# A macaron stack on one core: how the ternary FFN's weights are split and its chunks ordered, and attention's norm in two parts

## The reference

```
x = x + 0.5 * ffn(ln(x))     # w3(gelu(h2(gelu(h1(silu(w1 x s1) * (w2 x s2))))))
x = x + mamba(ln(x))         # selective scan, 256 channels, 16 states
x = x + 0.5 * ffn(ln(x))     # same weights
x = x + 0.5 * moe(ln(x))     # 16 experts, top 4, and a shared one
x = x + attn(ln(x))          # 16 heads of 64, outliers of the diagonal masked, two softmaxes
x = x + 0.5 * moe(ln(x))     # same weights as the moe above
```

## Time and profile before

| | us |
|---|---|
| median of 3 runs | 2042.3 |
| the profiled execution | 2039.14 |
| its span, first to last instruction | 2037.7 |
| of it PE busy | 1844.3 (91%) |
| DVE, POOL, ACT busy | 1374.8, 1183.9, 1124.5 |

### The profile page before, as it was taken

How to read it: one execution, slowest core, us unless ns; L and a number is a source line. 1 busy time by engine, 2 the same in 40 slices (tenths; PEclk the granted TensorE clock), 3 DMA queues, 4 the chain that set the end, 5 groups by cost and what they waited for, 6 DMA issues and landing times. The chain is left out here.

```text
span 2037.7 us, 21921 instructions
## 1 busy us (share of the span) xinstructions
PE 1844.3 (91%) x7360; PEld 1301.5 (64%) x7360; DVE 1374.8 (67%) x2202; ACT 1124.5 (55%) x1587; POOL 1183.9 (58%) x669
## 2 busy tenths in 40 slices
PE   5998999788997956999999999999999999998588
PEld 3773444335775634777777777777777777765266
DVE  5426899985517753677777777777777777774476
ACT  4326777744326445666566666665666566643444
POOL 2451777863444542466666666665757666668345
PEclk8999999999998978999999999999999999999799
DMA  2000000000001024132223231313131313100100
GB/s 93 0 1 0 0 0 0 1 0 1 0 4 43 1 50 103 34 76 48 67 44 71 43 72 39 76 42 74 38 76 39 76 38 75 38 12 11 52 6 16
DMA packets 46048, 74.51 MB, mean 37 GB/s; under 512 B 26864, under 2 KB 28528, under 8 KB 45680
## 3 DMA queue, kind: packets, MB, share of 16 engines
q1 hardware_dynamic: 43744, 72.35, 15.4%
q10 hardware_dynamic: 2160, 0.77, 0.1%
q0 software_dynamic: 32, 0.00, 0.0%
HBM read 20.93 MB, written 1.18 MB: 11 GB/s over the span
## 5 line engine op out<-in xcount | busy, mean ns | idle before, releaser
L2119 POOL TENSOR_TENSOR at_e_lo<-at_e,at_e_hi 128x1024 fp32r<-128x1024 f32 x256 | 614.7, 2402 | 377.3 <-DVE at_e_hi L2086 375.4
L1944 ACT ACTIVATE at_e<-at_ps 128x1024 f32<-128x1024 f32 x256 | 263.0, 1028 | 281.4 <-PE at_ps L1851 281.4
L1936 ACT ACTIVATE at_ps<-at_ps,at_neg_diag 128x1024 f32<-128x1024 f32 x256 | 278.6, 1088 | 89.2 <-DVE at_neg_diag L2004 89.2
L2011 DVE TENSOR_REDUCE at_row_max<-at_ps 128x1 f32<-128x1024 f32 x256 | 311.2, 1216 | 5.7 <-PE at_ps L1832 5.7
L2086 DVE CAST at_e_hi<-at_e 128x1024 fp32r<-128x1024 f32 x256 | 258.0, 1008 | 35.4 <-ACT at_e L1944 35.1
L2004 DVE CUSTOM_DVE_ANT_0 at_junk_diag<-at_ps,ident 128x128 bf16<-128x128 f32 x256 | 74.1, 290 | 258.8 <-PE at_ps L1805 258.7
L390 POOL TENSOR_TENSOR ffn_lo<-ffn_hid,ffn_hi 128x512 fp32r<-128x512 f32 x96 | 124.6, 1300 | 173.0 <-DVE ffn_hi L317 173.0
L1020 POOL TENSOR_TENSOR mb_work<-mb_work,mb_c 128x1024 f32<-128x1024 f32 x64 | 151.9, 2374 | 98.2 <-DVE mb_work L989 95.9
L1803 PE MATMUL at_ps<-at_k,at_q 128*128 128x512 f32 x512 | 162.0, 398 | 20.7 <-DMA at_k<-at_qk_lo 13.8
L1864 PE MATMUL at_pv_ps<-at_e_hi,at_v_hi 128*128 128x512 f32 x512 | 174.6, 422 | 0.3 <-ACT at_pv_sb L1960 0.3
L1832 PE MATMUL at_ps<-at_k,at_q 128*128 128x512 f32 x512 | 162.6, 399 | 11.3 <-DVE at_row_max L2011 8.0
(11 more groups left out here) (343 smaller groups left out, 3788.4 us busy)
## 6 DMA issues: line engine op xcount, KB each, us to landing
at_q<-at_qk_hi SPq DMA_DIRECT2D x64, 256.0 KB, 3.4
at_k<-at_qk_hi SPq DMA_DIRECT2D x32, 512.0 KB, 5.9
at_q<-at_qk_lo SPq DMA_DIRECT2D x32, 256.0 KB, 6.5
at_k<-at_qk_lo SPq DMA_DIRECT2D x32, 256.0 KB, 6.3
at_recips<-at_recip_row SPq DMA_DIRECT2D x32, 256.0 KB, 3.4
ffn_h_raw<-in_h SPq DMA_DIRECT2D x2, 1024.0 KB, 8.1
at_head_w_raw<-in_w_qkv SPq DMA_DIRECT2D x32, 64.0 KB, 4.2
x<-in_x SPq DMA_DIRECT2D x4, 256.0 KB, 4.8
```

Source lines behind the costliest of these rows:

```text
L1936: act.eng.activation(ps[:], ps[:], ACT.Exp, scale=SCALE, bias=m.small["neg_diag"][s][:, blk:blk + 1], accum_out=m.small["sums"][s][:, blk: ...
L1944: act.eng.activation(m.e[e % 2][:], slot("turned_scores", h, blk)[:], ACT.Exp, scale=SCALE).then_inc(sem["at_exp"])
L2011: dve.eng.tensor_reduce(m.small["row_max"][h % SLOTS][:, blk:blk + 1], slot("best", h, blk)[:], AX.X, ALU.max).then_inc(sem["at_best_out"])
L2119: pool.eng.tensor_tensor(m.e_lo[e % 3][:], m.e[e % 2][:], m.e_hi[e % 3][:].bitcast(F32), ALU.subtract).then_inc(sem["at_lo"])
```

## The change

The arithmetic stays the same; order, engines, queues and waits differ.

FFN, start: w1 and w2 are loaded from ACT's queue, right after the identity, and both are split by POOL (rounding and rest, two operations each). h1 is rounded by ACT after its norm work, and its rest made by POOL in four pieces. h2 and w3 are rounded by ACT after the first and third item of h1, and their rests made by DVE after the third and sixth. Mamba's loads move to SP's queue, behind the FFN's. PE waits for each matrix where it is first read. FFN, order (both FFNs): `j` is outside and `m` inside in every layer, in all the numberings too. DVE finishes and splits chunk 0 before it finishes chunk 1.

Attention: the first part centres all four chunks, and finishes, rounds and splits chunks 0 and 1; the main part then starts. The rest (inverse of chunk 3, finishing and splitting 2 and 3, the value weights) follows head 0's rounding on ACT and DVE, and on POOL it follows head 1's constant rows. PE waits in `project` and `values` for the chunks that they read. PSUM for the norm lies in the main part's banks, so two variances wait until an earlier one is read. SBUF tiles of the main part are allocated in another order.

```diff
 def ffn_u(t, first, m, j):
-    return t * FFN_U + first * KH + m * 2 + j
+    return t * FFN_U + first * KH + j * KH + m
...
 def ffn_pe(c, m_, t):
-    if t == 0:
-        pe.wait_ge(sem["ffn_w_lo"], len(c.ffn_parts))
     for first in range(0, NCH, 2):
-        for m in range(KH):
-            for j in range(2):
+        for j in range(2):
+            for m in range(KH):
                 pe.wait_ge(sem["ffn_xn_lo"], t * NCH + ch + 1)
+                pe.wait_ge(sem["ffn_in_parts"], 2)
...
+                pe.wait_ge(sem["ffn_in_parts"], 4)
...
+            if layer == 0:
+                pe.wait_ge(sem["ffn_in_parts"], 4 + KH)
+            else:
+                pe.wait_ge(sem["ffn_w_lo"], 2)
...
 def ffn_act(c, m_, t):
     if t == 0:
+        act.wait_ge(sem["ffn_h1_load"], 16)
+        act.eng.activation(c.ffn_parts["h1"][0][:], m_.raw["h1"][:], ACT.Copy).then_inc(sem["ffn_w_hi"])
         act.wait_ge(sem["ffn_load"], c.ffn_load_count)
-        for k, (hi, _) in c.ffn_parts.items():
-            act.eng.activation(hi[:], m_.raw[k][:], ACT.Copy).then_inc(sem["ffn_w_hi"])
...
+                    if t == 0 and first == 0 and layer == 0 and slot in FFN_LATE_HI:   # {0: "h2", 2: "w3"}
...
 def ffn_dve(c, m_, t):
     for j in range(2):
         norm_finish(dve, c, n0 + j, m_.norm_ps[j], m_.xn[j], m_.inv[j], m_.sq[j])
-    for j in range(2):
         split_xn(j, j)
...
+                    if t == 0 and first == 0 and layer == 0 and slot in FFN_LATE_LO:   # {2: "h2", 5: "w3"}
...
 def ffn_pool(c, m_, t):
     if t == 0:
-        pool.wait_ge(sem["ffn_w_lo"], len(c.ffn_parts))
+        pool.wait_ge(sem["ffn_in_load"], 2 * 16)
+        for i, k in enumerate(("w1", "w2")):
+            hi, lo = c.ffn_parts[k]
+            pool.eng.tensor_copy(hi[:], m_.raw[k][:]).then_inc(sem["ffn_in_parts"])
+            pool.wait_ge(sem["ffn_in_parts"], 2 * i + 1)
+            pool.eng.tensor_tensor(lo[:], m_.raw[k][:], hi[:].bitcast(F32), ALU.subtract).then_inc(sem["ffn_in_parts"])
+        hi, lo = c.ffn_parts["h1"]
+        pool.wait_ge(sem["ffn_w_hi"], 1)
+        for k in range(KH):
+            pool.eng.tensor_tensor(lo[:, k, :], m_.raw["h1"][:, k, :], hi[:, k, :].bitcast(F32),
+                                   ALU.subtract).then_inc(sem["ffn_in_parts"])
...
 def attention_norm_act(c, m):
+    load_logs(act)
+    for ch in range(2):
+        norm_square(act, c, 12 + ch, m.xn[:, COLS[ch]], m.inv[ch])
+    norm_square(act, c, 14, m.xn[:, COLS[2]], m.inv[2])
+    norm_inverse(act, c, 12, m.var_ps[0], m.inv[0], m.sq[0])
+    norm_inverse(act, c, 13, m.var_ps[1], m.inv[1], m.sq[1])
+    norm_square(act, c, 15, m.xn[:, COLS[3]], m.inv[3])
+    for ch in range(2):
+        attention_round_xn(c, m, ch)
+    norm_inverse(act, c, 14, m.var_ps[2], m.inv[2], m.sq[2])
+
+def attention_later_norm_act(c, m):
+    norm_inverse(act, c, 15, m.var_ps[3], m.inv[3], m.sq[3])
+    for ch in range(2, NCH):
+        attention_round_xn(c, m, ch)
     act.wait_ge(sem["attn_load"], 2 * 16)
     act.eng.activation(m.wv_hi[:], m.wv_raw[:], ACT.Copy).then_inc(sem["at_wv_hi"])
...
     act.wait_ge(sem["at_xn_lo"], NCH)
     act.wait_ge(sem["at_wv_lo"], 1)
...
+def attention_norm_dve(c, m):
+    for ch in range(NCH):
+        norm_centre(dve, c, 12 + ch, m.mean_ps[ch], c.x[:, COLS[ch]], m.xn[:, COLS[ch]])
+    for ch in range(2):
+        norm_finish(dve, c, 12 + ch, m.var_ps[ch], m.xn[:, COLS[ch]], m.inv[ch], m.sq[ch])
+    for ch in range(2):
+        attention_rest_of_xn(c, m, ch)
...
 def project(h):
+        pe.wait_ge(sem["at_xn_lo"], 2 * (h // HEADS) + 2)
...
         if at := due(t, AT_QK + 1):
             round_qk(at[0])
+            if at[0] == 0:
+                attention_later_norm_act(c, m)
```

More of the change, by code:

```diff
@@ L328, in ffn_dve @@
         dve.wait_ge(sem["ffn_load"], c.ffn_load_count)
[L329 to L334, removed]
+        dve.eng.tensor_scalar(c.half_s3[:], c.half_s3[:], 0.5, None, ALU.mult).then_inc(sem["ffn_w_lo"])
+        dve.wait_ge(sem["ffn_w_lo"], 1)
     for first in range(0, NCH, 2):
-        for m in range(KH):
-            for j in range(2):
+        for j in range(2):
+            for m in range(KH):
                 u, v = ffn_u(t, first, m, j), ffn_v(t, first, 0, m, j)
@@ L418, in ffn @@
         m.raw = {}
[L419 to L424 removed]
+        if t == 0:
+            for k, (hi, _) in c.ffn_parts.items():
+                m.raw[k] = sb(f"ffn_{k}_raw", hi.shape, F32)
+            for k in ("w1", "w2"):
+                nc.scalar.dma_start(m.raw[k][:], c.dram[k]).then_inc(c.sem["ffn_in_load"], 16)
+            nc.sync.dma_start(m.raw["h1"][:], c.dram["h1"]).then_inc(c.sem["ffn_h1_load"], 16)
+            for k in ("h2", "w3"):
+                nc.sync.dma_start(m.raw[k][:], c.dram[k]).then_inc(c.sem["ffn_load"], 16)
+                c.ffn_load_count += 16
+            for tile, name in c.mamba_loads:
+                nc.sync.dma_start(tile[:], c.dram[name]).then_inc(c.sem["mamba_load"], 16)
         m.parts = [[(sb(f"ffn_hi{layer}{j}", [P, KH, CH], F32R), sb(f"ffn_lo{layer}{j}", [P, KH, CH], F32R))
@@ L1607, in attention_norm_pe @@
 def attention_norm_pe(c, m):
[L1608 to L1623 removed]
+    pe, sem = c.pe, c.sem
@@ new lines, in attention_norm_pe, with attention_round_xn @@
+    for ch in range(3):
+        norm_mean(pe, c, m.mean_ps[ch], c.x[:, COLS[ch]])
+    for ch in range(2):
+        norm_variance(pe, c, 12 + ch, m.var_ps[ch], m.inv[ch])
+    norm_mean(pe, c, m.mean_ps[3], c.x[:, COLS[3]])
+    for ch in range(2, NCH):
+        pe.wait_ge(sem["norm_done"], 3 * (12 + ch - 2) + 1)
+        norm_variance(pe, c, 12 + ch, m.var_ps[ch], m.inv[ch])
+    pe.wait_ge(sem["norm_centred"], 12 + NCH)
+    pe.wait_ge(sem["at_xn_lo"], 2)
+def attention_round_xn(c, m, ch):
+    act, sem = c.act, c.sem
+    act.wait_ge(sem["norm_done"], 3 * (12 + ch) + 3)
+    act.eng.activation(m.xn_hi[:, COLS[ch]], m.xn[:, COLS[ch]], ACT.Copy).then_inc(sem["at_xn_hi"])
@@ L2112, in attention_pool @@
             fill_spare_rows(c, m, at[0])
+        if (at := due(t, AT_SPLIT)) and at[0] == 1:
+            attention_later_norm_pool(c, m)
         if at := due(t, AT_TURNED, BLK):
@@ L2152, in attention @@
         m.v_hi = sb("at_v_hi", [P, BLK, GROUP, 2, HD], F32R)
+        m.pv_ps = mem.enter_context(nc.psum_tensor("at_pv_ps", [P, 2 * CH], F32))
+        m.ps = [mem.enter_context(nc.psum_tensor(f"at_ps{i}", [P, 2 * CH], F32)) for i in range(3)]
+        m.mean_ps = [m.ps[ch // 2 * 2][:, HALF[ch % 2]] if ch >= 2 else m.pv_ps[:, HALF[ch]] for ch in range(NCH)]
+        m.var_ps = [m.pv_ps[:, HALF[ch % 2]] for ch in range(NCH)]
         with ExitStack() as early:
@@ L2158, in attention @@
             m.sq = [scratch[:, 1, COLS[ch]] for ch in range(NCH)]
-            m.banks = [early.enter_context(nc.psum_tensor(f"at_nps{i}", [P, CH], F32))[:] for i in range(8)]
             attention_norm_sp(c, m)
@@ L2236, in build, with later @@
         with ExitStack() as early:
+            def later(name, shape):
+                tile = sb(name, shape, where=early)
+                c.mamba_loads.append((tile, name))
+                return tile
             shapes = {"w1": [P, HID], "w2": [P, HID], "h1": [P, KH, HID], "h2": [P, KH, HID], "w3": [P, KH, P]}
```

151 lines of the change are left out of this document (73 added, 78 removed).

## The result

The changed kernel takes 2015.44 us, the median of 4 runs (2013.88 to 2017.08); the kernel before, timed beside it, 2043.79 (2041.71 to 2045.34). The ratio is 0.9862, 95% interval 0.9845 to 0.9879. The forecast was 2017, the range 2010 to 2027. By the medians 28.4 us are saved, where 25.5 were forecast. Run again on another chip with the experiments, the changed kernel took 2014.83 against 2042.19, 0.9869 (0.9853 to 0.9886).

The account below looks back on a forecast made before the run. PE's waits at the stage starts and for FFN splits were taken as the bound, attention's middle being PE-busy. Gains of 24.8 us plus about 0.7 for restarts, 25.5 off the 2042.3 median, gave 2017 us, range 2010 to 2027.

Parts of the forecast that it names:

- First FFN's start: First FFN: first gate product at 16.0 in place of 26.68, gate stage ending at 30.7 in place of 39.44, gaining 8.7 us.
- Rival A: First FFN's start: POOL and DVE disturb each other little, so it gains 2 more, 2015 us; chance 0.12.
- Rival B: First FFN's start gains less, since x arrives later or h1 comes late and holds ACT, 2022 us; chance 0.11.
- The table load's term: First FFN's norm: fewer DMA issues on ACT let the table load come earlier, giving 1.3 us.
- Squares: First FFN: squares of the next chunks, delayed by ACT's rounding of h2 and w3, cost 0.2 us.
- Three waits: First FFN: PE's three waits for POOL's `lo` of a hidden block go, 2.5 us.
- Second FFN: Second FFN: starting after chunk 0's split gives 2.1 us, and three waits for `lo` that go give 2.3.
- h2 and w3 later: First FFN: rounding and rests of h2 and w3, about 16 us per engine, hide beside 22.6 us of matmuls, cost zero.
- Attention: Attention's start: projection 0 starts at 744.6 against 752.87, after norming two chunks, gaining 8.2 us.
- Projection at full clock: Attention's start: PE stands still for only 2 us, so the projection's six matmuls run at full clock, saving 1.2 us.
- Room of 2.1 for the second half: Attention: the rest of the norm ends at 757.1, the first score can be read at 759.2, 2.1 us to spare.
- Rival C: Attention: the norm's second half overruns its gap by 5 us, with a cold clock, 2023 us; chance 0.10.

Follow-up runs that it names:

- pool_late: Changed kernel with one wait more: POOL makes the rests of h1 only when chunk 1's norm is split; 2012.21 us, ratio 0.9853 to the kernel before.
- q_act: Changed kernel with the fourteen mamba loads back on ACT's queue, behind w1 and w2, instead of SP's; 2018.05 us, ratio 0.9888 to the kernel before.
- u_order: Changed kernel with the FFN's blocks going in pairs of chunks again, in both FFNs; 2026.29 us, ratio 0.9928 to the kernel before.
- d_attn: Kernel before with only attention's part of the change: norm in two parts, tiles in their new places; 2031.81 us against 2041.08, ratio 0.9953.
- place: Kernel before with only the order in which attention's tiles take their places in SBUF changed; 2042.31 us against 2041.08, ratio 1.0003.
- warm1: Changed kernel with five unread matmuls in attention's norm, two ahead of variances, three ahead of the projection; 2013.82 us, ratio 0.9860 to the kernel before.
- slack: Changed kernel with nine unread DVE passes ahead of the second half of attention's norm; 2018.10 us, ratio 0.9884 to the kernel before.
- a_again: The changed kernel, unchanged, timed and profiled once more; 2014.83 us against 2042.19 for the kernel before, ratio 0.9869.
- combo: Changed kernel with POOL's h1 rests held until chunk 1 is split, and unread matmuls in attention's gaps; 2009.87 us, ratio 0.9849 to the kernel before.
- combo_f: Same as combo, with four more unread matmuls ahead of the first FFN's first gate matmul; 2009.10 us, ratio 0.9841 to the kernel before.

## Why the prediction was right

The mechanisms were right but for the clock of the projection, and the sum held: 24.8 and 0.7 forecast, 24.9 in the profiles, 28.4 by the medians. That the profiles' sum came out so close was luck: misses of both signs cancelled, 1.2 more in the first FFN, 1.9 more in mamba, 2.9 less in attention. By its own steps:

- **First FFN's start, 8.7.** First gate 15.77, chunk 1 split 22.7, first h1 matmul 30.51: 8.9. DVE and POOL took turns, as the step had it; pool_late shows that this is the cause, and worth 1.6 us. Rival A is refuted. POOL's rounding took 0.60, not 1.3, and nothing waited for it. Rival B did not come: chunk 1 is centred from 9.05 on (9.23 before), and ACT rounds h1 at 14.10, right behind its norm work, without a wait for the load. The table load's term (1.3) was 1.6 between the two profiles (chunk 0's inverse ends at 12.30, before at 13.89). It was too small against q_act (3.9) and the three other old starts, whose variances also ran at half clock.
- **Squares, 0.2.** Nothing: at the second variances the gain is 9.9.
- **Three waits, 2.5.** 12.2 at the end against 8.9 at the first h1 matmul: 3.3. The 0.8 more fit the 0.7 for restarts, which I added apart; no run separates them.
- **Second FFN, 4.4.** 4.27. The first gate matmul comes 2.0 us sooner behind mamba's last sum, and u_order brings the waits back (2.2). That matmul is at 460.3, not near 463.3: the 3.0 are mamba's 1.9 and the first FFN's 1.2.
- **h2 and w3 later, cover 16 of 22.6 us.** Held, but by the order: u_order pays 3.84 and a stretch at half clock. The prediction had counted the engines' time, not that DVE's rest of h2 and POOL's piece take turns.
- **Attention, 8.2.** 8.36 at the projection, 8.3 in d_attn against place.
- **Projection at full clock, 1.2.** The step that failed: 0.43 us apart as before, 0 gained. I had taken the last 2 us of idle time alone; but in the 6 us before the projection PE had only four matmuls, with idle times of 1.5, 1.0 and 1.8 before, between and behind them, and the granted clock fell at 725.5. With five fillers in these gaps (warm1) 1.1 of the 1.2 us are there.
- **Room of 2.1 for the second half.** slack: 2.1. Rival C did not come, and the room was placed right.
- **Not in the sum:** mamba 1.9 shorter. It was not touched, and this is a run's scatter; the profile before shows a granted clock of 0.89 in 165 to 180, the one after 1.00, and place, with the kernel before's mamba, has 1.00 there and a mamba 1.8 shorter too. In attention the gain is 8.1 us at the first diagonal, 9.6 at the first `e_hi` and 6.5 at the end: 1.7 us went to the slower pace, which a_again hasn't, and 1.3 to the one stretch at half clock at 1814 (0.91 in 1810 to 1830), which before hasn't. What sets the pace from run to run, and why the two come together, stays open.

## What to carry to other kernels

Start PE on what has landed, and order the blocks so that what is late is needed last; taking away either costs 11.5 to 12 us, but against d_attn the order alone gains 5.0 and the new start alone 5.5, and both about 17. Before giving an idle engine work, look at who shares its ports: POOL's passes beside a DVE chain from SBUF to SBUF made that chain 2.5 times as long (6.2 us for 2.5), and one wait on POOL gave 1.6 us back. One profile of each kernel can't tell 2 to 3 us: untouched stages differed by that much. A room is read from the last of the waits on an instruction, not from the idle time of its engine.

## What the runs showed of the hardware

- DVE's operations from SBUF to SBUF and POOL's two-input passes took turns. A DVE cast of 128x512 (0.43 us alone) that began beside a POOL pass ended 0.28 us after the pass, so it took up to 1.58; a POOL pass (1.3 alone) that began beside DVE's rest of 2.29 (128x2048) ended 1.15 after it and took 3.27.
- Matmuls that compute nothing, in PE's gaps of 1 to 10.7 us, kept the granted clock at 2.4 GHz where it had been 1.2: with 16 of them (combo, combo_f) the first diagonal came 2.2 us sooner. That the gain lasts behind it is not shown.
- ACT's fourteen DMA issues took 7.5 us in the profile of before and 8.5 in place, and the first gate matmul behind them came at 26.7 and 28.6.
